# A conditioned transformer block on one core: attention's RMS with tokens on partitions, its inverse sent as a row over DRAM

## The reference

```python
# 1. layer norm over the features, with a shift that depends on the sequence
out = (x - mean(x)) * rsqrt(var(x) + 1e-5) * weight + bias
x   = (out + tanh(cond @ lin_w.T + lin_b)[:, None]) * weight + bias
# 2. attention with 16 heads of 16, on an RMS norm whose scale and offset depend on the sequence
h = (cond @ gamma_w.T)[:, None] * x * rsqrt(mean(x * x) + 1e-6) + (cond @ beta_w.T)[:, None]
x = x + (cond @ alpha_w.T)[:, None] * attention(h)      # softmax over the 64 tokens of the sequence
# 3. a gated feed-forward part of width 1024, again behind such an RMS norm
h = (cond @ f_gamma_w.T)[:, None] * x * rsqrt(mean(x * x) + 1e-6) + (cond @ f_beta_w.T)[:, None]
x = x + (cond @ f_alpha_w.T)[:, None] * ((silu(h @ gate_w.T) * (h @ hidden_w.T)) @ out_w.T + out_b)
```

## Time and profile before

| | us |
|---|---|
| median of 3 runs (lowest, highest) | 967.99 (967.76, 968.27) |
| time of the profiled execution | 969.26 |
| its span, first to last instruction | 967.4 |

### The profile page before, as it was taken

The page is one execution under the profiler, slowest core; times in us unless marked ns, Lnnn a source line. Parts: engine busy times, 40 slices in busy tenths (PEclk is TensorE's granted clock), DMA queues, the critical chain, the costliest instruction groups (busy, mean ns, idle before and its releaser), DMA issues.

```text
span 967.4 us, 28344 instructions
## 1 busy us (share of the span) xinstructions
PE 932.0 (96%) x11164; PEld 896.9 (93%) x11164; DVE 717.1 (74%) x1355; ACT 616.8 (64%) x1732; POOL 582.4 (60%) x531
## 2 busy tenths in 40 slices
PE   5767999999999999999999999999999999999997
PEld 4757999999999999999999999999999999998997
DVE  5877787777878777777877777777777776677654
ACT  3566766766775766676676677667667666666432
POOL 4587657576674756757476675756666575544320
PEclk9799999999999999999999999999999999999999
DMA  7100010010000101010010101001000000000000
GB/s 228 57 2 24 2 32 16 13 34 13 24 13 14 34 13 35 2 35 13 13 34 14 34 2 35 13 13 34 13 23 13 13 13 12 13 13 13 13 12 22
DMA packets 20930, 23.33 MB, mean 24 GB/s; under 512 B 1216, under 2 KB 20288, under 8 KB 20800
## 3 DMA queue, kind: packets, MB, share of 16 engines
q1 hardware_dynamic: 20800, 21.54, 6.9%
HBM read 13.15 MB, written 8.39 MB: 22 GB/s over the span
## 4 chain that ended last, share of the span: by engine, by line
PE 91%; DVE 3%; POOL 2%; issue 2%; ACT 1%; DMA 0%; SPq 0%; DVEq 0%; ACTq 0%; POOLq 0%
PE psum L301 19%; PE psum L303 18%; PE psum L302 18%; PE psum L513 6%; PE psum L515 6%; PE psum L514 6%; PE psum L447 5%; PE psum L423 4%; PE psum L463 4%; PE psum L352 2%; PE psum L333 2%; PE psum L341 1%; PE psum L345 1%; POOL probs L1131 1%; DVE least L646 1%
## 5 line engine op out<-in xcount | busy, mean ns | idle before, releaser
L301 PE MATMUL psum<-xf_hi,ffn_hi 128*128 128x256 f32 x1024 | 289.7, 283 | 2.1 <-ACT probsT L929 1.8
L303 PE MATMUL psum<-xf_hi,ffn_lo 128*128 128x256 f32 x1024 | 286.0, 279 | 0.0
L302 PE MATMUL psum<-xf_lo,ffn_hi 128*128 128x256 f32 x1024 | 285.9, 279 | 0.0
L921 ACT ACTIVATE probs<-psum,least 128x64 f32<-128x64 f32 x928 | 206.3, 357 | 54.8 <-DVE least L646 54.1
L1131 POOL TENSOR_TENSOR probs<-probs,inv_sum 128x512 f32<-128x512 f32 x128 | 133.9, 1047 | 104.1 <-DVE inv_sum L667 103.4
L301 PEld LDWEIGHTS psum<-xf_hi,ffn_hi 128*128 128x128 f32 x1024 | 192.2, 188 | 3.3 <-issue 2.8
L303 PEld LDWEIGHTS psum<-xf_hi,ffn_lo 128*128 128x128 f32 x1024 | 192.4, 188 | 0.0
L302 PEld LDWEIGHTS psum<-xf_lo,ffn_hi 128*128 128x128 f32 x1024 | 192.0, 188 | 0.0
L950 ACT ACTIVATE prod_hi<-late 128x512 fp32r<-128x512 f32 x128 | 84.2, 658 | 115.1 <-DVE late L725 114.8
L513 PE MATMUL psum<-prod_hi,ffn_hi 128*128 128x256 f32 x512 | 143.3, 280 | 0.9 <-DVE prod_lo L731 0.9
L717 DVE SCALAR_TENSOR_TENSOR late<-tanh,psum 128x512 f32<-128x512 f32 x128 | 86.7, 677 | 76.9 <-ACT tanh L944 76.9
(11 more groups left out here) (103 smaller groups left out, 2207.0 us busy)
## 6 DMA issues: line engine op xcount, KB each, us to landing
out_t_dram<-x_res SPq DMA_DIRECT2D x31, 256.0 KB, 2.2
xin<-x_dram SPq DMA_DIRECT2D x15, 512.0 KB, 4.0
w_raw<-attn_w_dram SPq DMA_DIRECT2D x1, 1024.0 KB, 8.9
x_res<-gate_w_dram SPq DMA_DIRECT2D x1, 1024.0 KB, 11.5
late<-hidden_w_dram SPq DMA_DIRECT2D x1, 1024.0 KB, 13.0
w_raw<-out_w_dram SPq DMA_DIRECT2D x1, 1024.0 KB, 6.4
xin<-x_dram SPq DMA_DIRECT2D x2, 256.0 KB, 3.0
k_heads<-mod_w_dram SPq DMA_DIRECT2D x1, 320.0 KB, 4.0
```

Source lines behind the costliest of these rows:

```text
L301: pe.matmul(out, stat_hi, mov_hi, start=first, stop=False)
L302: pe.matmul(out, stat_hi, mov_lo, start=False, stop=False)
L303: return pe.matmul(out, stat_lo, mov_hi, start=False, stop=last)
L921: op = act.activation(probs[g % 4][:, h * SEQ:(h + 1) * SEQ], scores[g % 2][:, h // 2, h % 2], ACT.Exp, bias=least[g % 2][:, h:h + 1], sca ...
```

## The change

From part 6 on (block 3 and later) the layer norm's multiplication and shift, and the mean square of attention's norm, are done while tokens are still on partitions. The shift differs by sequence, so it is needed as rows: once, at step 1, TensorE turns w*w and the shift of all sequences into rows in bank 0, ScalarE copies them out, and SyncE stores the shift rows to DRAM at step 2. For each tile SyncE loads the shift rows of its two sequences, each spread over 64 partitions (`load_shift`). VectorE applies mean, w*w, inverse deviation and shift in two instructions (`shift_tokens`). ScalarE squares the tile and sums along the partition in the same instruction (`square_tokens`). After `turn_x` ScalarE, not VectorE, copies the bank to the residual (`residual_out`). The two columns of mean squares get the epsilon on VectorE (`token_squares_out`) and the power on GpSimd (`token_inverse`), SyncE writes them to a row of 256 numbers in DRAM and reads the row back over all partitions (`send_inverses`), and `scale_a` multiplies by it. Gone for these parts: `normalise_tokens`, `make_residual`, `square_a`, `sum_squares_a`, and the two transposes each of `turn_squares` and `spread_inverses`. Tiles 0, 1 and 2 of a block are shifted at the end of VectorE's steps j = 1, 2, 3 of the odd group before the block is turned; the fourth is shifted in the even group's step j = 1, behind `mean_squares_out` and `product_lo`.

```diff
+ROW_FROM = 6
+        def turns_a(grp):
+            return is_part(grp + 2) and grp + 2 < ROW_FROM
+        def tile_at(s):
+            b, k = divmod(s + 11, 2 * PSEQ)
+            if not ROW_FROM // 2 <= b < NBLK or k not in (0, 1, 2, 4):
+                return None
+            return 4 * b + min(k, 3)
         def norm_cols(grp, n):
-            return slice(0 if is_part(grp + 2) else 2 * n, 4 * n if is_part(grp - 2) else 2 * n)
+            return slice(0 if turns_a(grp) else 2 * n, 4 * n if is_part(grp - 2) else 2 * n)
...
+            def load_shift(i):                                   # SyncE
+                n = tile_no(i)
+                if n == 0:
+                    sp.wait_ge(table_sent, 16)
+                if n >= 2:
+                    sp.wait_ge(y_tok, n - 1)
+                for h in range(2):
+                    sp.dma_start(shift_tok[n % 2][h * SEQ:(h + 1) * SEQ],
+                                 shift_rows[2 * i + h:2 * i + h + 1].partition_broadcast(SEQ)).then_inc(shift_loaded[n % 2], 16)
+            def send_inverses(m):
+                p = m - ROW_FROM
+                sp.wait_ge(token_inv_made, p + 1)
+                for i in range(2):
+                    sp.dma_start(inv_rows[p % 2, i * P:(i + 1) * P].unsqueeze(1), token_inv[:, p % 2 * 2 + i:p % 2 * 2 + i + 1]
+                                 ).then_inc(inv_sent, 16)
+                sp.wait_ge(inv_sent, 32 * (p + 1))
+                if p >= 1:
+                    sp.wait_ge(scaled_a, m)
+                sp.dma_start(inv_row[:], inv_rows[p % 2:p % 2 + 1].partition_broadcast(P)).then_inc(row_loaded, 16)
...
+                if s == 2:
+                    sp.wait_ge(rows_made, 1)
+                    sp.dma_start(shift_rows, rows[:, D:2 * D]).then_inc(table_sent, 16)
+                if tile_at(s + 1) is not None:
+                    load_shift(tile_at(s + 1))
+                if s % PSEQ == 0 and row_part(s // PSEQ + 2):
+                    send_inverses(s // PSEQ + 2)
...
             def turn_squares(grp):                               # TensorE
-                if is_part(grp + 2):
+                if turns_a(grp):
+            def turn_rows():
+                pe.wait_ge(shift_made, 3)
+                pe.wait_ge(mod_out, 2)
+                for kt in range(KT):
+                    pe.transpose(gate_bank[:, kt * P:(kt + 1) * P], w_sq[:, kt:kt + 1].broadcast_to([P, P]), ident[:])
+                for kt in range(KT):
+                    mm = pe.transpose(gate_bank[:, (KT + kt) * P:(KT + kt + 1) * P], mod[:, SHIFT, kt], ident[:])
+                mm.then_inc(rows_mm, 1)
...
                 if s == 1:
                     keys(1)
+                    turn_rows()
...
+            def shift_tokens(i):                                 # VectorE
+                b, k, n = i // TILES, i % TILES, tile_no(i)
+                x_tile = xin[b % 2][:, k]
+                ...
+                dve.scalar_tensor_tensor(out=x_tile, in0=x_tile, scalar=mean[b % 2][:, k:k + 1], in1=w_sq_row,
+                                         op0=ALU.subtract, op1=ALU.mult).then_inc(centred, 1)
+                dve.wait_ge(centred, n + 1)
+                dve.wait_ge(shift_loaded[n % 2], 32 * (n // 2 + 1))
+                dve.scalar_tensor_tensor(out=x_tile, in0=x_tile, scalar=rstd[b % 2][:, k:k + 1], in1=shift_tok[n % 2][:],
+                                         op0=ALU.mult, op1=ALU.add).then_inc(y_tok, 1)
+            def token_squares_out(m):
+                ...
+                dve.tensor_scalar(token_inv[:, cols], token_ms[:, cols], RMS_EPS, None, ALU.add).then_inc(token_ms_out, 1)
             def scale_a(m):
+                dve.wait_ge(gamma_a, m + 1)
+                if row_part(m):
+                    dve.wait_ge(row_loaded, 16 * (m - ROW_FROM + 1))
+                    dve.tensor_tensor(normed_a[:], normed_a[:], inv_row[:].unsqueeze(1).broadcast_to([P, KT, PART]),
+                                      ALU.mult).then_inc(scaled_a, 1)
+                    return
                 dve.wait_ge(inv_spread, m + 1)
...
                 if is_step(f - 1):
                     product_lo(f - 1)
+                if j == 0 and row_part(grp + 2):
+                    token_squares_out(grp + 2)
+                if j == 1 and tile_at(s) is not None and tile_at(s) % TILES == 3:
+                    shift_tokens(tile_at(s))
...
                 if j == 3 and is_part(grp - 2):
                     ffn_split_lo(grp - 2)
+                if tile_at(s) is not None and tile_at(s) % TILES < 3:
+                    shift_tokens(tile_at(s))
...
+            def square_tokens(i):                                # ScalarE
+                n = tile_no(i)
+                act.wait_ge(y_tok, n + 1)
+                ...
+                act.activation(squares_a[:, 0], xin[i // TILES % 2][:, i % TILES], ACT.Square, scale=ROOT_D,
+                               accum_out=token_ms[:, n % 4:n % 4 + 1]).then_inc(sq_tok, 1)
+            def residual_out(m):
+                ...
+                act.wait_ge(x_turned, m + 1)
+                act.activation(res_part(m), by_kt(norm_bank), ACT.Copy).then_inc(res_made, 2)
...
+                if tile_at(s - 1) is not None:
+                    square_tokens(tile_at(s - 1))
                 if j == 0 and is_part(grp - 2) and s > FFN_AT:
                     square_f(grp - 2)
+                if j == 0 and row_part(grp + 2):
+                    residual_out(grp + 2)
...
+            def token_inverse(m):                                # GpSimd
+                ...
+                pool.tensor_tensor(token_inv[:, cols], token_inv[:, cols], minus_half[:, cols], ALU.pow
+                                   ).then_inc(token_inv_made, 1)
```

More of the change, by code:

```diff
@@ L125, in conditioned_block @@
         gated_a = sb("gated_a", [P, KT, PART])
+        rows = sb("rows", [P, 2 * D])
+        w_sq_row = rows[:, 0:D]
+        shift_tok = [sb(f"shift_tok{i}", [P, D]) for i in range(2)]
+        token_ms = sb("token_ms", [P, TILES])
+        token_inv = sb("token_inv", [P, TILES])
+        inv_row = sb("inv_row", [P, PART])
+        shift_rows = nc.dram_tensor("shift_rows", [BATCH, D], F32).ap()
+        inv_rows = nc.dram_tensor("inv_rows", [2, PART], F32).ap()
         squares_f = sb("squares_f", [P, KT, PART])
@@ L172, in conditioned_block @@
         out_mm, gated_f_made, y_made = sem("out_mm"), sem("gated_f_made"), sem("y_made")
+        rows_mm, rows_made, table_sent = sem("rows_mm"), sem("rows_made"), sem("table_sent")
+        shift_loaded = [sem(f"shift_loaded{i}") for i in range(2)]
+        centred, y_tok, sq_tok, token_ms_out = sem("centred"), sem("y_tok"), sem("sq_tok"), sem("token_ms_out")
+        token_inv_made, inv_sent, row_loaded = sem("token_inv_made"), sem("inv_sent"), sem("row_loaded")
         last_gated, last_made = sem("last_gated"), sem("last_made")
@@ L316, in norm_bank_read @@
                     pe.wait_ge(ms_read, grp + 3)
-                if j == 2 and is_part(grp + 2):
+                if j == 2 and turns_a(grp):
                     pe.wait_ge(scaled_a, grp + 3)
@@ L329, in turn_x @@
             def turn_x(m):
-                pe.wait_ge(x_normed, m + 1)
+                if row_part(m):
+                    pe.wait_ge(y_tok, tile_no(2 * m + 2))
+                else:
+                    pe.wait_ge(x_normed, m + 1)
                 for i in range(2):
@@ L428, in turn_bank_free @@
                 grp = (g + 2) // PSEQ
+                if g == 1:
+                    pe.wait_ge(rows_made, 1)
                 if g % 2 == 1:
@@ L804, in _ @@
                     scale_a(0)
-                if j == 0 and is_part(grp + 2) and not PSEQ <= s <= FFN_AT:
+                if j == 0 and is_part(grp + 2) and not PSEQ <= s <= FFN_AT and not row_part(grp + 2):
                     make_residual(grp + 2)
@@ L858, in square_a @@
                 act.activation(squares_a[:], res_part(m), ACT.Square, scale=ROOT_D).then_inc(squared_a, 1)
+            def square_tokens(i):
+                n = tile_no(i)
+                act.wait_ge(y_tok, n + 1)
+                if n == 0:
+                    act.wait_ge(sq_sum_a, ROW_FROM)
+                if n >= 4:
+                    act.wait_ge(token_ms_out, n // 2 - 1)
+                act.activation(squares_a[:, 0], xin[i // TILES % 2][:, i % TILES], ACT.Square, scale=ROOT_D,
+                               accum_out=token_ms[:, n % 4:n % 4 + 1]).then_inc(sq_tok, 1)
+            def residual_out(m):
+                if m // 2 == 3:
+                    act.wait_ge(ffn_lo_made, split_no(3))
+                if m % 2 == 0 and m // 2 >= RES:
+                    act.wait_ge(stored[m // 2 % RES], 16 * 2 * (m // 2 // RES))
+                act.wait_ge(x_turned, m + 1)
+                act.activation(res_part(m), by_kt(norm_bank), ACT.Copy).then_inc(res_made, 2)
             def square_f(m):
@@ L1016, in _ @@
                         exponentials(s + 1)
```

(16 more changed lines are left out.)

24 lines of the change are left out of this document (20 added, 4 removed).

## The result

The changed kernel takes 959.85 us (median of 4 runs, 959.70 to 962.56) against 967.88 (4 runs, 967.32 to 968.27) for the kernel before on the same chip: a ratio of 0.9923, 95% interval 0.9909 to 0.9936. It is 8.0 us faster, where 8.5 was forecast, and 0.35 us above the forecast of 959.5. The profiled execution took 959.94 (span 958.1); its partner before took 969.26 (span 967.4).

The account below looks back on a forecast made before the run. The prediction took TensorE, full behind the start, to bound the kernel. Its terms, -11.4 + 0.9 + 2.0 = -8.5 us, took the median from 967.99 to 959.5 us; forecast range 956.5 to 962.5 (chance 0.60), wider range 955.5 to 967.0.

Parts of the forecast that it names:

- Removed, -11.4 us: TensorE, parts 6 to 31: four transposes fewer in each of 26 parts, at 0.11 us each.
- Rival D: All of the upper saving (0.145 us for L352's transposes) and no stall: -13.3 + 0.5, 955.2 us; chance 0.06.
- Start, +0.9 us: Step 1: four added transposes at 0.2 us each stand on the path; bounds 0 and 1.5 us.
- Rival C: The start gets longer, another stretch running at TensorE's slow pace: 3 to 4 us more, 963 us; chance 0.08.
- Place one: Even group, step j = 0: third tile's shift delays VectorE's minima 1.05 us; slack falls to about 0.1 us, no stall.
- VectorE's lateness, +2.0 us in all: TensorE stalls from VectorE's order of work in 13 blocks: 0.15 us a block; bounds 0 and 13.7 us.
- Place two: Even group, step j = 1: fourth tile in front of invert_sums; stall 0 to 0.1 us, up to 0.97 more.
- ScalarE and GpSimd: In each part ScalarE gets about 0.7 us more work, within idle time; GpSimd only gets lighter.
- The row over DRAM: Inverses written and read back: writes land after 2.5 us, row arrives 406.5 to 408, slack 5 us or more.
- rival B: Row late for scale_a in 26 parts, from a 14.5 us trip on; about 980 us at 15.5; chance 0.09.

Follow-up runs that it names:

- p4: The changed kernel with the four transposes of each of the 26 parts put back as identity transposes that nobody reads; 971.24 us, ratio 1.0044.
- p7: The changed kernel with its new path only from part 18 on, the old path below it, so 14 parts instead of 26; 965.16 us, ratio 0.9971.
- p3: The kernel before with only the four transposes at step 1, ScalarE's copy of the rows and the table's store; 967.44 us, ratio 1.0001.
- p10: The changed kernel with the pair of writes of the inverses made twice before the row is read; 1205.18 us, ratio 1.2459.

## Why the prediction was right, step by step

**Removed, -11.4 us: right.** 0.11 us a transpose from the distance of starts, not the 0.287 of the mean. p4 measured 11.4, p7 0.43 a part. Rival D's 0.145 for the spread inverses doesn't hold: the change over from the score matmuls stays, as L415's two at 0.36 us show beside L352's four at 0.58.

**Start, +0.9 us: not seen.** p3 measured 0.1, between -0.8 and 1.0. The term took the 0.2 us of a transpose as the pace of this stage; it was that of the lower clock, which after's execution doesn't have there. Rival C isn't seen.

**Place one: right to 0.2 us.** The groups are to be laid over one another by their first turn, 397.52 before and 393.00 after, so 4.52 us are taken off the forecast's times. VectorE in after, and the instruction of GpSimd that it meets:

```profile
391.58 1.50 DVE L703 SCALAR_TENSOR_TENSOR xin<-xin,mean,rows 128x256 f32<-128x256 f32 x1
393.11 0.48 DVE L707 SCALAR_TENSOR_TENSOR xin<-xin,rstd,shift_tok 128x256 f32<-128x256 f32 x1
393.52 0.68 DVE L833 TENSOR_TENSOR prod_lo<-late,prod_hi 128x512 fp32r<-128x512 f32 x1
394.12 0.16 DVE L716 TENSOR_SCALAR token_inv<-token_ms 128x2 f32<-128x2 f32 x1
394.19 1.28 DVE L743 TENSOR_REDUCE least<-psum 128x8 f32<-128x512 f32 x2
...
399.65 0.69 DVE L827 TENSOR_TENSOR late<-psum,late 128x512 f32<-128x512 f32 x1
```

```profile
391.07 1.72 POOL L1275 TENSOR_TENSOR x_res<-x_res,gated_a 128x512 f32<-128x512 f32 x1
```

The second instruction of the shift was forecast to end at 393.4 and ends at 393.59; the epsilon at 394.18, and ends at 394.28; the minima at 395.48, and end at 395.47; the product at 400.33, and ends at 400.34. TensorE turns the square sums at 400.71, so there is no stall and 0.37 us of slack. As forecast, the first instruction of the shift now takes the blow that `prod_lo` took the earlier trace rows: 1.50 us behind GpSimd's L1275, 0.48 where nothing is in its way. One reading was wrong: the first tile of a block was said not to be behind a GpSimd instruction, but in 12 of 13 blocks L703 meets L1279 there and takes 1.20 to 1.22 us. The idle time covers it, as forecast.

**VectorE's lateness, +2.0 us in all: the size right, the spread not.** It is not 0.15 us in each block. Place one costs nothing in the steady groups, but about 1 us once, in the first group with the new order, where VectorE also splits a piece of the feed-forward's weights (L861 at 111.78, 0.69 us) in the same queue: that group takes 29.11 us, and its chain of waits runs over L703, L861, `prod_lo` and the minima to ScalarE's copies of the keys, until TensorE goes on at 117.33. In p7, where the new order begins long after that splitting, its first group takes 28.10. Place two costs 0.03 us in most blocks and 0.1 in one. Together about 1.5 us.

**ScalarE and GpSimd: right in sum, though one price was missed.** ScalarE's squares cost 419 + 195 ns each, since the sum along a row is read out by an instruction of its own. By the page's busy times ScalarE takes (634.9 - 616.8) / 26 = 0.7 us more a part, as forecast, VectorE 0.9 (717.1 to 740.5) where 0.7 was forecast, and GpSimd 3.1 less (582.4 to 501.0). All of it is hidden.

**The row over DRAM: right that it is in time, wrong by how much.** The step that fails is the 2.5 us for the landing of a write, taken from a DMA with a packet for each partition. Measured it is 7 us and more until the read can go, and the read takes 4.8 in the median (3.0 to 6.0) instead of 2.5 to 4.0. The row comes at 407.0 where 402.0 to 403.5 was forecast (406.5 to 408, less 4.52), and the slack is 0.3 to 2.0 us instead of 5. The text named 14.5 us as the trip from which rival B decides; the trip is 407.0 - 394.1 = 12.9 here, and 12.6 to 14.4 over the 26 parts. That no part was late is luck as much as reckoning. The sentence of the Trainium skill that stood beside rival B (DMA: Bandwidth & Descriptors, section Anatomy of one DMA — SWDGE (gpsimd) path), on completions of writes to HBM, agrees with the 7.7 us here. The fixed cost of about 2.0 us that the section gives, for DMAs that GpSimd issues, would be far too little for these, which SyncE issues.

**Not in the prediction: +2.6 us for the places of buffers.** 0.08 us a group (p7's old path against before) for 32 groups. It is larger than the forecast's whole term for VectorE. With the 1.5 us above it makes 4.1 of the 4.3 us that p4 measured for all but the transposes.

The sum by what was measured: -11.4 + 0 + 1.5 + 2.6 = -7.3 us, against -8.0. What is left, 0.7 us, is within what the start scatters. The mechanism, four transposes out of a full TensorE, was right. That the number agrees to 0.35 us is partly luck: +2.6 that wasn't seen is cancelled by a start 0.9 cheaper than forecast, a VectorE term 0.5 cheaper, and those 0.7.

## What to carry to other kernels

Where TensorE is the bound, price what it loses by the distance of starts in the chain, and lay the waits of one group out in time before trusting that the work moved elsewhere is hidden. Ask of each new buffer which moving operands it pushes: 32 bytes cost 9.8 us here, and 64 may have won 3, so a change's gain should be compared at the same places, and the places tried by themselves. A trip over DRAM with short writes needs its own measurement, and whoever moves its wait moves everything that its queue holds behind it. Price a wait of TensorE with the slower clock that may follow it.

## What was not expected of the hardware

- The distance of fp32 matmuls of 128x256 depends on where in SBUF their moving operand lies: with the clock granted in full 117.7, 118.6 and 119.8 ns at displacements of 0, 64 and 32 by 256 against `xf_hi` of the kernel before, and 113.4 or 117.8 at 128. `xf`, `prod`, `xn` and `att` each follow their own place. Four remainders were tested.
- Two writes of 128 x 4 bytes to DRAM took 7.0 to 10.6 us from issue to the read that waits for them, in all kernels that send them once. What in them takes the time was not separated.
- Behind waits of TensorE of about 6 us (p10) the granted clock was at 1.2 GHz for 3.4 to 10.2 us, and a part took 3.6 us more than the wait explains.
- GpSimd's short power (L1203, 402.06 to 403.15) did not hold VectorE up: L703 starts at 402.50 and takes 0.48 us. GpSimd's L1275 on 128x512 numbers did, 1.50 instead of 0.48. The Trainium skill (SBUF — State Buffer, section SBUF: two separate sides) gives the shared ports to whichever starts first for its whole length. The long instruction agrees. So does the power's own length: it starts inside VectorE's L833 (401.89 to 402.58) and takes 1.09 us, where the same power (L1210) takes 0.71 beside L743, which has one input. That L703 then runs beside it at its usual length does not agree. Of the 0.97 us that the prediction feared for place two nothing is seen.
